# Stacks of keys and queries three partitions apart, and a new order of the lead-in in the three cross-attentions

## What is computed

```python
Q = _split_heads(tokens @ Wq)          # 16 heads of 16
K = _split_heads(context @ Wk)
V = _split_heads(context @ Wv)
scores = jnp.einsum('bhnd,bhmd->bhnm', Q, K) * SCALE
attn = jax.nn.softmax(scores, axis=-1)
out = jnp.einsum('bhnm,bhmd->bhnd', attn, V)
...
x = x + _L3_xattn_ref(_layernorm(x, axis=-1), ctx_768, ...)
```

## Time and profile before

| | us |
|---|---|
| median of three runs | 2535.56 (2533.76 to 2538.5) |
| the profiled execution | 2525.97 |
| its span in the trace | 2524.3 |
| PE busy | 2225.2 (88%) |
| DVE busy | 1240.3 (49%) |
| ACT busy | 1044.0 (41%) |
| queue 1 (SP's and ACT's DMAs), share of 16 engines | 22.1% |

### The profile page before, as it was taken

The page is one execution under the profiler, slowest core; times in us unless marked ns, Lnnn a source line. Parts: engine busy times, 40 slices in busy tenths (PEclk is TensorE's granted clock), DMA queues, the critical chain, the costliest instruction groups (busy, mean ns, idle before and its releaser), DMA issues. The chain is left out here.

```text
span 2524.3 us, 42831 instructions
## 1 busy us (share of the span) xinstructions
PE 2225.2 (88%) x13610; PEld 1643.9 (65%) x13611; DVE 1240.3 (49%) x2762; ACT 1044.0 (41%) x2555; POOL 535.8 (21%) x556
## 2 busy tenths in 40 slices
PE   8998399569998999898898998999997499989998
PEld 5664298444565874466785664679997256568887
DVE  4664300369876329876434664100000456577764
ACT  1564133214565523466532663124443036654332
POOL 1000200310122430121551000220001410054443
PEclk9999699789999999999998999999999699999999
DMA  7771143110000000000008741123221386110001
GB/s 190 154 173 70 46 169 109 46 42 0 26 0 15 26 17 0 25 0 3 13 6 143 133 79 74 36 106 121 73 106 47 99 154 129 36 34 20 26 25 34
DMA packets 110836, 164.29 MB, mean 65 GB/s; under 512 B 15273, under 2 KB 95257, under 8 KB 105721
## 3 DMA queue, kind: packets, MB, share of 16 engines
q1 hardware_dynamic: 101712, 140.68, 22.1%
q0 software_dynamic: 7680, 20.98, 2.6%
q10 hardware_dynamic: 1320, 1.03, 0.2%
HBM read 114.96 MB, written 47.32 MB: 64 GB/s over the span
## 5 line engine op out<-in xcount | busy, mean ns | idle before, releaser
L1043 DVE TENSOR_REDUCE xa_mx<-ps 128x2 f32<-128x512 f32 x384 | 247.0, 686 | 100.6 <-PE ps L695 99.5
L141 PE MATMUL ps<-ones 128*128 128x384 f32 (+1 forms) x450 | 164.7, 495 | 98.6 <-DMA ex_rows<-rows_out,rows_back 37.7
L902 ACT ACTIVATE xn_tok<-ps 128x512 f32<-128x512 f32 x384 | 210.6, 602 | 52.6 <-PE ps L703 50.4
L1482 PEld LDWEIGHTS ps<-ex_xT,ex_w 128*128 128x128 f32 x1792 | 210.5, 193 | 7.2 <-issue 4.4
L1482 PE MATMUL ps<-ex_xT,ex_w 128*128 128x128 f32 x1792 | 211.1, 276 | 3.8 <-issue 3.8
L1489 PE MATMUL ps<-ex_w,ex_h 128*128 128x256 f32 x896 | 202.7, 379 | 0.0
L141 PEld LDWEIGHTS ps<-ones 128*128 128x128 f32 x450 | 91.0, 223 | 142.9 <-issue 49.9
L695 PE MATMUL ps<-xa_ks,xa_qs 48*128 48x256 f32 (+1 forms) x768 | 157.7, 323 | 27.7 <-DMA xa_qs<-x_queries 9.1
L2147 PE MATMUL ps<-lo_w,lp_hs 128*128 128x512 f32 x384 | 176.1, 610 | 4.5 <-ACT lp_hs L2194 2.8
L1489 PEld LDWEIGHTS ps<-ex_w,ex_h 128*128 128x128 f32 x896 | 165.9, 190 | 20.2
L695 PEld LDWEIGHTS ps<-xa_ks,xa_qs 48*128 48x128 f32 (+1 forms) x768 | 106.6, 192 | 102.0 <-DVE xa_mx L1043 52.2
(11 more groups left out here) (343 smaller groups left out, 4815.8 us busy)
## 6 DMA issues: line engine op xcount, KB each, us to landing
xa_ks<-x_keys SPq DMA_DIRECT2D x144, 128.0 KB
xa_qs<-x_queries SPq DMA_DIRECT2D x144, 128.0 KB, 4.6
ex_w<-in_L0f_w_dram SPq DMA_DIRECT2D x16, 1024.0 KB, 7.0
ex_w<-in_L2f_w_dram SPq DMA_DIRECT2D x16, 1024.0 KB, 6.8
x_keys<-xa_khl SPq DMA_DIRECT2D x24, 512.0 KB, 5.6
x_queries<-xa_qhl SPq DMA_DIRECT2D x24, 512.0 KB, 3.0
ex_stage<-rows_in POOLq DMA_DIRECT2D x64, 128.0 KB, 2.3
rows_out<-ex_rows SPq DMA_DIRECT2D x56, 128.0 KB, 1.7
```

The costliest lines, as they stand in the source:

```text
L141: self.nc.tensor.matmul(self.ps[:, bank, 0:wide * P], self.ones[:], self.ones[:].unsqueeze(1).to_broadcast([P, wide, P]), start=True, stop ...
L902: nc.scalar.activation(pT[:, h % SLOTS].rearrange("p k q -> p (k q)"), c.ps[:, S_BANK + (HEADS * b + n) % 3], ACT.Exp).then_inc(exped.sem, 1)
L1043: nc.vector.tensor_reduce(mx[:, half, :, col], c.ps[:, M_BANK + h % 2].rearrange("p (t n) -> p t n", t=2), AX_X, ALU.max).then_inc(max_put ...
L1482: ins = nc.tensor.matmul(c.ps[:, f % 4, 0:P], w1[:, buf, k, f * P:(f + 1) * P], xT[:, k], start=(k == 0), stop=(k == KD - 1))
```

## The change

The diff does five things.

1. The columns of Wq and Wk (and their biases) are laid out by `by_row` when the inputs are prepared, so that a projected row belongs to (half, row, head) and no longer to (head, half, row). In DRAM the 128 KB of one stack are then one contiguous block, 8 KB for each of 16 partitions.
2. A stack writes the partitions `64 * j + n`, then every third one (`ks[at:at + 3 * HD - 2:3, ...]`), and no longer 16 neighbours. The rows of the three groups interleave; the sum over them is the same.
3. `stack_keys` and `stack_queries` take the engine and the half. In the lead-in SP issues the lower halves of batches 0 and 1, ACT the upper halves. From batch 2 on, SP issues both.
4. In the lead-in SP stacks the lower keys of a batch before it sends that batch's queries. The load of `wo` moves behind the query stacks of batch 1.
5. Each half has its own semaphores, so PE waits for four where it waited for two, once for a batch.

```diff
-    K_LOADS = 6 + 2 * masked
+    K_LOADS, Q_LOADS = 3 + masked, 3
...
+        def stack_keys(eng, j, b):
+            eng.wait_ge(*k_sent(16 * b + 16))
+            if b >= K_BUFS:
+                eng.wait_ge(*scored_T(HEADS * (b - K_BUFS + 1)))
+            parts = dram["x_keys"][b].rearrange("(a j r g) t -> a j r g t", a=2, g=PAIRS, j=2)
+            for n, part in enumerate((0, 0, 1)):
+                at = 64 * j + n
+                eng.dma_start(ks[at:at + 3 * HD - 2:3, b % K_BUFS].bitcast(F32), parts[part, j]
+                              ).then_inc(k_in[j][b % 3].sem, 16)
...
+        def stack_queries(eng, j, b):
+            eng.wait_ge(*q_sent(16 * b + 16))
...
-            def stack_keys(b):
-                sp.wait_ge(*k_sent(16 * b + 16))
...
-                parts = dram["x_keys"][b].rearrange("(a g j r) t -> a j r g t", a=2, g=PAIRS, j=2)
-                for j in range(2):
-                    for n, part in enumerate((0, 0, 1)):
-                        at = 64 * j + HD * n
-                        sp.dma_start(ks[at:at + HD, b % K_BUFS].bitcast(F32), parts[part, j]
-                                     ).then_inc(k_in[b % 3].sem, 16)
...
             send_keys(0)
-            send_queries(0)
             if masked:
                 sp.wait_ge(*rows_masked(2))
-            stack_keys(0)
-            stack_queries(0)
-            sp.dma_start(wo[:], dram[tag + "wo"]).then_inc(loaded.sem, 16)
+            stack_keys(sp, 0, 0)
+            send_queries(0)
+            stack_queries(sp, 0, 0)
             if masked:
                 lo, hi = CTX_PARTS[1]
                 sp.dma_start(c.ctxT[:, :, lo:hi], dram["ctxT"][:, :, lo:hi]).then_inc(ctx_in[1].sem, 16)
             send_keys(1)
+            stack_keys(sp, 0, 1)
             send_queries(1)
-            stack_keys(1)
-            stack_queries(1)
+            stack_queries(sp, 0, 1)
+            sp.dma_start(wo[:], dram[tag + "wo"]).then_inc(loaded.sem, 16)
             send_keys(2)
-            stack_keys(2)
+            stack_keys(sp, 0, 2)
+            stack_keys(sp, 1, 2)
...
                         if n == 0:
-                            pe.wait_ge(*k_in[(b + 1) % 3](16 * K_LOADS * ((b + 1) // 3 + 1)))
-                            pe.wait_ge(*q_in[(b + 1) % 2](16 * 6 * ((b + 1) // 2 + 1)))
+                            for j in range(2):
+                                pe.wait_ge(*k_in[j][(b + 1) % 3](16 * K_LOADS * ((b + 1) // 3 + 1)))
+                                pe.wait_ge(*q_in[j][(b + 1) % 2](16 * Q_LOADS * ((b + 1) // 2 + 1)))
...
             lead_keys(0)
             put_rows(0)
+            if masked:
+                act.wait_ge(*rows_masked(2))
+            stack_keys(act, 1, 0)
             lead_queries(0)
             lead_keys(1)
+            stack_queries(act, 1, 0)
             put_rows(1)
+            stack_keys(act, 1, 1)
             lead_queries(1)
+            stack_queries(act, 1, 1)
             put_values(0)
...
+    def by_row(w):
+
+        return w.reshape(w.shape[:-1] + (HEADS // 2, 2, HD)).swapaxes(-3, -2).swapaxes(-2, -1).reshape(w.shape)
```

More of the change, by code:

```diff
@@ L479, in xattn_phase @@
     k_sent, q_sent, rows_set = c.sig("keys_sent"), c.sig("queries_sent"), c.sig("rows_set")
-    k_in = [c.sig("first_keys_in"), c.sig("second_keys_in"), c.sig("third_keys_in")]
-    q_in = [c.sig("even_queries_in"), c.sig("odd_queries_in")]
+    k_in = [[c.sig(n + part + "keys_in") for n in ("first_", "second_", "third_")] for part in ("", "upper_")]
+    q_in = [[c.sig(n + part + "queries_in") for n in ("even_", "odd_")] for part in ("", "upper_")]
     max_sent = [c.sig("lower_max_sent"), c.sig("upper_max_sent")]
@@ L524, in xattn_phase @@
         S_BANK, M_BANK, O_BANK, Y_BANK, W_BANK = 0, 3, 5, 6, 7
+        def stack_keys(eng, j, b):
[8 more added lines that the diff above has]
+            if masked:
+                at = 64 * j + 3 * HD
+                eng.dma_start(ks[at:at + 1, b % K_BUFS].bitcast(F32),
+                              mbias[:, b * S:(b + 1) * S].bitcast(F32).unsqueeze(1).to_broadcast([1, PAIRS, S])
+                              ).then_inc(k_in[j][b % 3].sem, 16)
+        def stack_queries(eng, j, b):
+            eng.wait_ge(*q_sent(16 * b + 16))
+            if b >= Q_BUFS:
+                eng.wait_ge(*scored_T(HEADS * (b - Q_BUFS + 1)))
+            parts = dram["x_queries"][b].rearrange("(a j r g) t -> a j r g t", a=2, g=PAIRS, j=2)
+            for n, part in enumerate((0, 1, 0)):
+                at = 64 * j + n
+                eng.dma_start(qs[at:at + 3 * HD - 2:3, b % Q_BUFS].bitcast(F32), parts[part, j]
+                              ).then_inc(q_in[j][b % 2].sem, 16)
         @block.gpsimd
@@ L636, in _ @@
                     send_queries(b + 2)
-                    stack_queries(b + 2)
+                    for j in range(2):
+                        stack_queries(sp, j, b + 2)
                 if b + 3 < B:
                     send_keys(b + 3)
-                    stack_keys(b + 3)
+                    for j in range(2):
+                        stack_keys(sp, j, b + 3)
                 if masked:
@@ L1127, in xattn_phase @@
     for n in range(3):
-        k_in[n].spent(16 * K_LOADS * len(range(n, B, 3)))
+        for j in range(2):
+            k_in[j][n].spent(16 * K_LOADS * len(range(n, B, 3)))
     for par in range(2):
-        q_in[par].spent(16 * 6 * (B // 2))
+        for j in range(2):
+            q_in[j][par].spent(16 * Q_LOADS * (B // 2))
         max_sent[par].spent(16 * B)
@@ L2865, in _layouts @@
     o["ctxT"][KC[1], 1] = 1.0
+    def by_row(w):
+        return w.reshape(w.shape[:-1] + (HEADS // 2, 2, HD)).swapaxes(-3, -2).swapaxes(-2, -1).reshape(w.shape)
     for tag, src in (("L0x_", "L0_xattn_"), ("L2x_", "L2_xattn_"), ("L3x_", "L3_xattn_")):
         for name in ("Wq", "Wk", "Wv", "Wo"):
-            o[tag + name.lower()] = _chunked(a[src + name])
-    o["L2x_wk"][KC[1], 1] = a["L2_xattn_bk"]
+            w = a[src + name]
+            o[tag + name.lower()] = _chunked(by_row(w) if name in ("Wq", "Wk") else w)
+    o["L2x_wk"][KC[1], 1] = by_row(a["L2_xattn_bk"])
     o["L2x_wv"][KC[1], 1] = a["L2_xattn_bv"]
-    o["L2x_qcol"] = a["L2_xattn_bq"].reshape(KD, P).T
+    o["L2x_qcol"] = by_row(a["L2_xattn_bq"]).reshape(KD, P).T
     o["L2x_bo"], o["L3x_bo"] = a["L2_xattn_bo"].reshape(1, 1, D), a["L3_xattn_bo"].reshape(1, 1, D)
```

21 lines of the change are left out of this document (3 added, 18 removed).

## The result

| | us |
|---|---|
| kernel before, median of 15 runs | 2533.11 (2527.23 to 2539.78) |
| changed kernel, median of 15 runs | 2543.94 (2538.7 to 2552.4) |
| ratio, with its 95% interval | 1.0044 [1.0031, 1.0057] |
| profiled execution, before and after | 2525.97 and 2541.28 |

The account below looks back on a forecast made before the run. PE was taken as the busiest engine, transfers mattering only where PE waits. Lead-ins +5.7, -1.1 and -1.1, loop waits -5 and clock -4 gave -5.5 us on a median of 2535.56: 2530.0 us, range 2521 to 2542.

Parts of the forecast that it names:

- part 2: Third lead-in: ACT waits for the second key store; `wo` late, +0.4 us, keys' remainder wait gone, -1.5: -1.1 us.
- Part 5: Loops over batches: -5 us from fewer waits for maxima, -4 us from a higher granted clock.
- the sum of the lead-ins: The three cross-attention lead-ins before their loops: +5.7 us in the first, -1.1 in the second, -1.1 in the third.
- its term s: Price of one 128 KB stack issued from two queues: 0.45 us taken, between bounds of 0.33 and 1.0 us.
- the prediction's formula: Stack price from drain time: take off 0.6 us to start, 1.3 for the query store, 1.4 to confirm.
- Key stacks are gone by then: Third lead-in: key stacks drained before the first query store, issued at 2014.0, lands at 2016.9 us.
- bound of 0.6: Upper bound in us for one DMA issue, seen on ACT for another shape; 0.45 us was taken.
- the 2.85 us: Third lead-in: PE's wait before its first score in the kernel before, of which 1.8 us were to come back.
- The signs: Observations named beforehand as showing the forecast right or wrong, such as twelve stacks over 7 us from two queues.
- part 4: First lead-in: second key store lands at 38.0 us, first maximum 46.4, values 50.7; +5.7 us in all.
- the halves don't run side by side: Rival on stacks from two queues: price near 0.7 us, lead-ins longer, 2546 us, slower; chance 0.17.
- Its turning point: Stack price of 0.6 us, from which the kernel would be slower, the sum passing +2 us.

Follow-up runs that it names:

- order_only: Changed kernel with the old stack layout (16 neighbouring partitions, 1 KB pieces), keeping the new lead-in order and ACT's issues: 1.0106 of the kernel before.
- pieces_only: Kernel before with contiguous 8 KB pieces and permuted columns, but still 16 neighbouring partitions and the old order: 1.0049 of the kernel before.
- layout_only: Kernel before with the new stack layout alone, old order, SP issuing all: 0.992 of the kernel before; 0.9933 when run again.
- cast_first: Changed kernel with ACT's second query cast moved ahead of its wait for the second key store, `wo` still late: 1.0046 of the kernel before.
- spread_only: Kernel before with every third partition as target but the old 1 KB pieces, SP in the old order: 0.9936 of the kernel before.
- one_queue: Same as `act_aside_2`, but SP also issues batch 0's upper halves and ACT issues no stacks: 0.9902 of the kernel before, 2505.18 us.
- act_aside_2: New layout; ACT issues only batch 0's upper halves, behind casts; `wo` early, rest of context behind second stores: 0.9913 of the kernel before, 2508.5 us.

## Why the prediction was wrong

**The mechanisms of the lead-in were right.** The new wait stood where part 2 put it, at the second key stacks, with ACT's cast, DVE's remainder, statistics and maxima behind; `wo` ended last in the second and third.

**Part 5 had the right sum, and its two terms missed in opposite directions.** The three loops, from the first `score_T` of each to its last, are 59.23 to 218.41, 1370.49 to 1525.51 and 2046.35 to 2197.52 us before, and 67.35 to 221.69, 1383.28 to 1535.18 and 2063.09 to 2213.75 after. Their sums, length first and then each engine's busy time:

```profile
sum 465.37, PE 442.73 PEld 297.31 DVE 294.03 ACT 296.49 POOL 12.73; mean PE 147.57 PEld 99.10 DVE 98.01 ACT 98.83 POOL 4.24
...
sum 456.90, PE 437.33 PEld 294.21 DVE 294.18 ACT 296.26 POOL 12.73; mean PE 145.78 PEld 98.07 DVE 98.06 ACT 98.75 POOL 4.24
```

PE stands idle for 19.6 us where it was 22.6, and needs 5.4 us less for the same matmuls, at a granted clock of 0.99, 1.00 and 0.99 in the three loops where it was 0.97, 0.99 and 0.98. So the loops gave 3 us by waits and 5.4 by the clock, for a forecast of 5 and 4. The waits for maxima there fell from 6.4 us to 3.2 only; the second of the two large ones is still there, with 2.17 us at 191.00.

The medians say the same. Take their difference and subtract that of the lead-ins: for the ten kernels with every third partition -3.6 to -12.1 us are left for the rest of the program, -9.3 on average (-9.2 for the changed kernel); for `order_only` -2.4, and for `pieces_only` +5.8. Each rests on one traced execution, and the two looks at the same `layout_only` differ by 6 us.

**The step that failed is the sum of the lead-ins, +3.5 forecast and +20.0 measured, above all by its term s, the price of a stack from two queues.** The third, from its first key store (issued at 2008.53 in the prediction, at 2018.45 in the trace after), us:

| | forecast | measured |
|---|---|---|
| first key store landed | 2.8 | 3.2 |
| first query cast | 4.2 | 5.4 |
| first query store issued | 5.5 | 6.7 |
| landed | 8.4 | 10.6 |
| second key store issued | 9.9 | 12.4 |
| landed | 14.4 | 17.6 |
| second query cast | 15.8 | 19.7 |
| second query store issued | 17.1 | 21.1 |
| landed | 20.0 | 24.3 |
| `wo` landed | 25.2 | 31.6 |

The rows of SP and ACT behind the measured column:

```profile
2018.45 0.38 SPq L605 DMA_DIRECT2D x_keys<-xa_khl  x1
2021.65 2.06 SPq L533 DMA_DIRECT2D xa_ks<-x_keys  x3
2025.19 0.39 SPq L610 DMA_DIRECT2D x_queries<-xa_qhl  x1
2029.01 1.76 SPq L548 DMA_DIRECT2D xa_qs<-x_queries  x3
2030.81 0.58 SPq L605 DMA_DIRECT2D x_keys<-xa_khl  x1
2036.05 1.75 SPq L533 DMA_DIRECT2D xa_ks<-x_keys  x3
2039.52 0.36 SPq L610 DMA_DIRECT2D x_queries<-xa_qhl  x1
2042.79 1.75 SPq L548 DMA_DIRECT2D xa_qs<-x_queries  x3
2044.58 0.58 SPq L626 DMA_DIRECT2D xa_wo<-in_L3x_wo_dram  x1
...
2021.65 1.78 ACTq L533 DMA_DIRECT2D xa_ks<-x_keys  x3
2023.86 0.59 ACT L874 CAST xa_qhl<-ps 128x512 fp32r<-128x512 f32 x1 [4.03 <-issue]
...
2029.01 2.03 ACTq L548 DMA_DIRECT2D xa_qs<-x_queries  x3
2031.09 0.59 ACT L856 COPY xn_T<-ps 128x512 f32<-128x512 f32 x1 [3.25 <-issue]
2036.06 2.03 ACTq L533 DMA_DIRECT2D xa_ks<-x_keys  x3
2038.18 0.59 ACT L874 CAST xa_qhl<-ps 128x512 fp32r<-128x512 f32 x1 [6.51 <-issue]
```

A cast stands in the table with its start, a landing with the issue of what waits for it; `wo` lands by PE's values at 2050.05. Of the 6.4 us too few, three issues ahead of each cast or store make 1.8 (0.8, 0.3 and 0.7), the landings 4.5 (0.4, 0.9, 0.7, 0.4 and 2.1). The 0.7 at the second cast costs nothing by itself, as `cast_first` showed. So two terms were mis-sized, the first above all:

- *The price of a stack from two queues.* By the prediction's formula the second key store gives (36.05 - 29.01 - 3.3) / 6 = 0.62 us, and `wo` (50.05 - 42.79 - 2.65) / 6 = 0.77; the first attention, with the context's 3.8 us, gives (41.07 - 28.67 - 7.1) / 6 = 0.88 (0.85 with the 4.0 us that 1536 KB take at 390 GB/s). The forecast took 0.45, from the context load, and one queue alone has 0.81 in `spread_only`. "Key stacks are gone by then" was wrong for the same reason: the first query store takes 3.8 us, not 2.9.
- *The issue.* 0.59 us on SP and 0.61 on ACT, not 0.45. The bound of 0.6 was named and then left aside; that bound, another DMA into `ks` issued by ACT, was the right row.

**A third step was left out, and a fourth came out otherwise.** The forecast charged +0.35 us to PE's chain up to the first score. But `put_rows(1)` stands on ACT behind the first query stacks, whose store lands late: its copy is at 2031.09, 12.6 us behind the key store, where it was 9.3 behind it before. PE's fillers then end only at 2038.81, and that is why the first score comes 20.36 us after the key store (20.31 before) although no stack is waited for: nothing of the 2.85 us came back. This cost no time of its own here, since PE then stood 6.57 us for `wo`.

Behind the values part 2 took off 1.5 us for the wait for the keys' remainder. That wait did fall, from 1.52 to 0.19 us, but from the values to the loop it is 13.04 us where it was 13.06. The eight matmuls of the values, right behind PE's pause, ran at a granted clock of 0.50, the lower level, and took 3.78 us; before it was 2.68 us at 0.74. The forecast had no term for the clock behind a new pause.

**First lead-in.** Forecast: store landed at 38.0, first maximum at 46.4, values at 50.7. Measured 41.07, 50.14 and 54.99, with starts that lie 0.7 us earlier than before. The second key store is 3.1 us late, by the dearer stacks; the rest of that chain (issues, cast, statistics) took 9.07 us where 8.35 were forecast. The values come 11.85 us later behind the first key store than before, where 6.9 were forecast. From the values to the loop 3.1 us came back, more than the 1.25 of the forecast.

**The signs.** Of those named for a wrong forecast two were met: twelve stacks take over 7 us from two queues (12 x 0.62 = 7.4 at the least), and PE's first score of the first attention comes before 41 us, at 38.23. The second tells nothing: part 4 gives no time for that score, and it was at 39.16 before.

**Which rival it was.** The second: the halves don't run side by side, s near 0.7, 2546 us. It came true with its mechanism, the key stacks that delay the query stores behind them, and with its size (2543.94), and it had a chance of 0.17. Its lead-ins would be 18.3 us longer (3.5 + 14.8), 20.0 were measured, and its rest -8, for -9.2. The closeness is partly luck: the dearer issues, ACT's late copy and the clock behind the new pauses weren't in it. Its turning point, slower from s = 0.6 on, agrees with 0.62 to 0.88 and a slower kernel; nothing ran near 0.6 to test it. What stood against it, 390 GB/s for the context load, compares a transfer over 128 partitions with one over 16; the runs have the new pattern at 0.78 to 0.81 us from one queue and 0.62 to 0.88 from two. The Trainium skill ("DMA: Bandwidth & Descriptors", Rules for kernel authors) has two transfers to disjoint halves serialise; `one_queue` beside `act_aside_2` nearly agrees, 0.78 us a stack to 0.65 and 2505.18 us to 2508.5. The other page, "SBUF — State Buffer" of the Trainium skill (Door 1: The DMA port swizzle), had the direction: more ports reached, cheaper stack, 0.81 us for 0.95 from one queue. The prediction's estimate of 0.4 us from it doesn't hold: two queues have 0.62 to 0.88. Nor does the page's figure of 27.2 GB/s a port give it: an estimate from that is 0.6 us for a stack alone on eight ports, and 0.3 for each of two side by side.

## What to carry to other kernels

When a DMA's issue moves onto a compute engine, write down what stands behind its wait on that engine, and then what else ends at the same time: two waits side by side hide each other, and an experiment that removes one can show nothing, as `cast_first` did. A value chosen between bounds that are a factor of three apart should not lean on a transfer of another shape; where the sign turns inside the bounds, as here at 0.6 of 0.33 to 1.0 us, the chances should be spread accordingly. Test the parts of a change singly: this one was a gain of 0.8% and a loss of 1.1% in one diff.

## What the runs showed that I had not expected

- The cost of issuing a 128 KB DMA depends on the target: 0.42 to 0.43 us with 16 neighbouring partitions, 0.59 to 0.60 with every third, whatever the piece size (0.600 with 1 KB, 0.589 with 8 KB), on the same engine. On ACT it is 0.61 with every third partition and 0.45 with neighbours (`order_only`).
- Pieces of 8 KB in place of 1 KB don't speed up a stack (0.96 and 0.95 us) and with 16 neighbours as the target PE waits longer for the maxima, which come by another queue: 13.0 us, not 7.2. With every third partition it doesn't (1.8 us in `layout_only`, 2.3 in `spread_only`).
- PE pauses from 39.58 to 50.89 us in the first attention. The granted clock is 0.93 from 40 to 45 us and 0.50, the lower level, from 45 to 55 (windows above). In the kernel before it was 0.63, 0.69 and 0.66 in those three windows, behind a pause of 2.38 us, with PE busy nearly throughout. A part of the low clock now falls into the pause, where it costs nothing, and from the values to the loop the changed kernel needs 12.4 us where the one before needed 15.4; 0.8 us of that is less idle time ahead of the loop.
